# The last tile list takes 24 tiles in place of 18, and six early read-backs and their adds are issued inside the tail

## The reference

```python
def _L0_gnn_ref(h, adj, W_w, W_b, a):
    Wh = h @ W_w + W_b
    e = leaky_relu((Wh @ a1)[:, None] + (Wh @ a2)[None, :], negative_slope=0.2)
    attention = softmax(where(adj > 0, e, NEG), axis=1)
    return attention @ Wh
def _L0_ffn_ref(x, Wg, bg, W1, b1, W2, b2):
    topk_scores, topk_idx = top_k(x @ Wg.T + bg, 2)
    topk_probs = softmax(topk_scores)
    ...
    out = out + combine[..., e:e + 1] * (relu(x @ W1[e].T + b1[e]) @ W2[e].T + b2[e])
x = x + _L0_gnn_ref(_layernorm(x), adj, ...)
x = x + _L0_ffn_ref(_layernorm(x), ...)
```

## Time and profile before

| what | value |
|---|---|
| median of 3 runs | 413.72 us (413.57 to 413.85) |
| profiled execution, its own time | 413.95 us |
| its span | 412.2 us |
| TensorE busy | 383.2 us, 93% of the span |
| VectorE, ScalarE, GpSimd busy | 295.3, 270.1, 204.3 us |
| moved by DMA | 116.44 MB, mean 282 GB/s |
| granted TensorE clock, mean | 0.989 |

### The profile page before, as it was taken

How to read it: one execution, slowest core, us unless ns; L and a number is a source line. 1 busy time by engine, 2 the same in 40 slices (tenths; PEclk the granted TensorE clock), 3 DMA queues, 4 the chain that set the end, 5 groups by cost and what they waited for, 6 DMA issues and landing times.

```text
span 412.2 us, 8417 instructions
## 1 busy us (share of the span) xinstructions
PE 383.2 (93%) x2434; PEld 257.1 (62%) x2434; DVE 295.3 (72%) x819; ACT 270.1 (66%) x451; POOL 204.3 (50%) x247
## 2 busy tenths in 40 slices
PE   1899999999999999999999999999989999999960
PEld 1545555444444444444366667798879999999960
DVE  5998896989799979899988696268951692111173
ACT  1589879675878666892376975458646666676630
POOL 3283451100401874206763058789787777555560
PEclk9999999999999999999999999999999999999995
DMA  6999998969959999898676994576577777667795
GB/s 197 358 425 373 344 353 251 422 250 374 384 220 305 354 302 408 322 319 328 185 244 236 380 316 145 184 245 219 191 231 237 251 239 240 218 222 240 243 361 184
DMA packets 45610, 116.44 MB, mean 282 GB/s; under 512 B 7517, under 2 KB 19682, under 8 KB 38902
## 3 DMA queue, kind: packets, MB, share of 16 engines
q1 hardware_dynamic: 37062, 100.02, 68.0%
q0 software_dynamic: 4320, 8.47, 6.2%
q10 hardware_dynamic: 4176, 7.34, 5.9%
HBM read 84.57 MB, written 13.07 MB: 237 GB/s over the span
## 4 chain that ended last, share of the span: by engine, by line
PE 75%; DMA 8%; DVE 6%; issue 4%; SPq 3%; ACT 2%; POOL 2%; ACTq 0%; POOLq 0%; DVEq 0%
PE acc L1600 46%; PE acc L1702 10%; DMA adj<-adjT 3%; PE hps L1684 3%; PE hps L1686 3%; PE hps L1685 3%; PE yt L1702 3%; DVE prob L971 2%; PE yt L1645 2%; DMA ybuf<-wst,dest 1%; DMA adj<-ybuf 1%; PE pj L1721 1%; PE pj L1558 1%; SPq L547 1%; PE yt L1567 1%
## 5 line engine op out<-in xcount | busy, mean ns | idle before, releaser
L1600 PE MATMUL acc<-prob,Wh 128*128 128x512 f32 (+1 forms) x576 | 236.0, 550 | 3.8 <-DVE prob L971 2.7
L971 DVE SCALAR_TENSOR_TENSOR prob<-s_bc,E_col,G_all 128x1024 f32<-128x1024 f32 (+2 forms) x159 | 169.7, 1096 | 21.9 <-PE acc L1600 18.5
L1600 PEld LDWEIGHTS acc<-prob,Wh 128*128 128x128 f32 x576 | 103.5, 190 | 98.8 <-issue 84.2
L1355 ACT ACTIVATE G_all<-adj 128x2048 bf16<-128x2048 int32 (+1 forms) x67 | 119.0, 1800 | 22.7 <-DMA adj<-adjT 12.8
L784 POOL DMA_INDIRECT xbuf<-xr,slot x64 | 72.6, 1135 | 49.6 <-PE acc L1600 30.5
L800 POOL DMA_INDIRECT ybuf<-wst,dest x71 | 73.2, 1031 | 45.4 <-ACT wst L1438 25.0
L1702 PE MATMUL acc<-wall,prob 128*128 x368 | 51.1, 282 | 0.0
L1702 PEld LDWEIGHTS acc<-wall,prob 128*128 128x128 f32 x368 | 44.7, 192 | 0.2
L1223 DVE COPY share<-slab 128x1 f32<-128x1 f32 x45 | 6.8, 155 | 47.1 <-DMA slab<-xbuf 44.5
L1428 ACT ACTIVATE prob<-hps 128x512 f32<-128x512 f32 x46 | 27.6, 599 | 6.5 <-PE hps L1686 1.4
L1438 ACT ACTIVATE wst<-acc,share 128x128 f32<-128x128 f32 x45 | 16.6, 368 | 17.3 <-PE acc L1702 15.6
(11 more groups left out here) (249 smaller groups left out, 554.0 us busy)
## 6 DMA issues: line engine op xcount, KB each, us to landing
adj<-adjT SPq DMA_DIRECT2D x52, 1024.0 KB, 8.1
adj<-adjT SPq DMA_DIRECT2D x16, 768.0 KB, 6.2
s_bc<-wall SPq DMA_DIRECT2D x47, 256.0 KB
wlb<-wall SPq DMA_DIRECT2D x24, 256.0 KB
slab<-xbuf SPq DMA_DIRECT2D x71, 65.0 KB
adj<-ybuf SPq DMA_DIRECT2D x6, 512.0 KB, 7.7
xs<-x SPq DMA_DIRECT2D x8, 256.0 KB, 10.5
wst<-wcat ACTq DMA_DIRECT2D x8, 256.0 KB, 4.2
```

Source lines behind the costliest of these rows:

```text
L971: nc.vector.scalar_tensor_tensor(prob[n % PR][:, 0:w], c_bc[:, P * AT[g]:P * AT[g] + w], E_col[:, u:u + 1], G[m % GR][:, k * w:(k + 1) * w ...
L1355: nc.scalar.activation(G[m % GR][:, 0:w], adj_sb[m % AR][:, 0:w], ACT.Relu).then_inc(s_G, 1)
L1600: last = nc.tensor.matmul(bank[:, 0:k * P], Wh[:, u, :], prob[n % PR][:, b * P:(b + k) * P], start=(u == 0), stop=(u == TILES - 1), skip_g ...
```

## The change

The number of tiles in the list before the last goes from 12 to 6, so the last list begins with tile 47 and holds 24 tiles. `OLD` becomes the number of tiles that the first 24 blocks can fill at most, 55 in place of 61. The scratch table of the last list (24 by 24) moves to `G_all`, where the attention masks lay. The six early read-backs are issued by SyncE in its beats 60 to 65, one in each, behind that beat's slab and weight copy; the first one's wait for the given-back tiles goes with it. VectorE's adds for these parts are written into its beats 65 to 70.

```diff
     SURE = [-((E * (P - 1) - 2 * P * (AT[g] + WB[g])) // P) for g in range(SG - 1)]
     NT = (2 * N + E * (P - 1)) // P
     SURE[0] = 0
+    OLD = (2 * P * AT[SG - 2] + E * (P - 1)) // P
+    SURE[SG - 2] = OLD - E
+    assert OLD - E - SURE[SG - 3] >= 2 * AT[SG - 2] - SURE[SG - 3] - 1
     FIRST = [0] + SURE + [NT]
     CNT = [FIRST[r + 1] - FIRST[r] for r in range(SG)]
     MOST = max(CNT)
     CAP = N + P
     SPARE = NT - 2 * N // P
     C = 3 * E
-    OLD = FIRST[SG - 1] + E
     OLDER = (2 * P * AT[SG - 1] + E * (P - 1)) // P
     ROWS = E * CAP + SPARE * P
 
@@ -179,7 +181,8 @@
         WxT = WT
         full, acum = cut(0, E, TILES), cut(0, C, C)
...
-                       [cut(base, n, w) for base, n, w in ((544, MOST, E), (544, CNT[-2], 2 * E), (CNT[-1] * C, CNT[-1], C))])
+                       [cut(base, n, w) for base, n, w in ((544, MOST, E), (544, CNT[-2], 2 * E))])
+        pastq.append(G_all[:, 0:2 * CNT[-1] * C].bitcast(fp32).rearrange("p (a b) -> p a b", b=C))
...
-            def first_reads():
-
-                given_back(OLD)
-                for c in range(SOON):
-                    read_back(c)
+            def first_read(c):
+
+                if c == 0:
+                    given_back(OLD)
+                read_back(c)
...
                     for t in copies_at.get(n, ()):
                         copy_weights(t)
+                    for c in range(SOON):
+                        if n == beat_step[OLD + 5 + c]:
+                            first_read(c)
...
                 main(False)
-                first_reads()
...
-            def add_all():
-                for c in range(len(last_pass)):
+            def add_rest():
+                for c in range(SOON, len(last_pass)):
                     add_up(c)
...
                                 if t < NT:
                                     target(t)
+                            if 0 <= k - OLD - 10 < SOON:
+                                add_up(k - OLD - 10)
...
                 main(False)
-                add_all()
+                add_rest()
```

## The result

The changed kernel takes **416.78 us** (median of 8 runs, 414.83 to 418.99) against 413.71 for the kernel before (8 runs beside it, 412.51 to 414.78): the ratio is 1.0067, with a 95% interval of 1.0048 to 1.0087. It is slower by 0.5 to 0.9%. The forecast was 411.5; the kernel became slower, as rival (c) had it.

A forecast was written before the change was run, and what follows sets the result against it. TensorE was taken to bound the tail, then DMA work and a slow last give-back the final 14 us. From 413.72 us, -2.4 (end) + 0.2 (TensorE's wait) + 0 + 0 = -2.2 gave 411.5; range 410.3 to 413.4.

The forecast's parts named there:

- rival (c): Tail, slab 70 and copies behind it: TensorE starves and the kernel gets slower, 415.0 us; chance 0.08.
- The end, -2.4 us: After the last scaling: with early reads gone, the last two reads start at 403.0 instead of 405.4, gaining 2.4 us.
- The give-back is slow because of the six early read-backs: Tail's end: six reads issued from 387.16 on were said to make the give-back from 394.03 take 5.96 us.
- the median, 3.3 us: Last give-back: its landing time taken as the median of indirect writes without that load, range 2.5 to 4.7 us.
- rival (a): End: stores and ScalarE's three reads alone keep the last give-back at 5.3 us; 413.3 us, chance 0.13 together with (d), reads starting no earlier.
- TensorE's wait, +0.2 us: Turn of tile 70: its slab lands late behind four reads; TensorE waits 0 to 1.3 us once, taken as 0.2.
- near the lower end, because the SyncE queue itself goes slower: Tile 70's wait: 0.2 chosen from 0 to 1.3 us, since fewer rounds would be ahead of its slab.
- The rule of the Trainium skill: DMA queues: engines alternate between rows but take one row in ring order, so SyncE's slabs and copies wait behind reads.
- SyncE's issue times: Tail: wait for tile 54 costs nothing, first read issued about 378.5, last slab 386.5, all six reads by about 389.
- The adds: VectorE: six parts' adds, some 8.6 us, hidden before the next parts land from about 401 on; cost 0.
- The lists: Longer last table adds 1.1 us on VectorE, covered; slab 47's later wait costs 0, at most 1 us.
- the step on the earlier trace: Shorter table: VectorE feeds TensorE up to 0.7 us sooner, ending in the weight-copy wait at 303.44; counted 0.

The follow-up runs named there:

- e0: The changed kernel once more, unaltered, for a second profile; 416.49 us, ratio 1.0069 to the kernel before.
- e2: Changed kernel with all slabs up to tile 70 loaded ahead of the first early read-back; 416.66 us, ratio 1.0081 to the kernel before.
- e3: Changed kernel with the six early read-backs sent from ScalarE's DMA queue, one a beat, instead of SyncE's; 418.34 us, ratio 1.0112 to the kernel before.
- e7: Changed kernel without the six stores of the first 24 tiles; 416.69 us, ratio 1.0073 to the kernel before.
- e11: Changed kernel with early reads cut to an eighth of their bytes and the six early stores left out; 413.30 us, ratio 0.9986 to the kernel before.
- e12: Changed kernel with eighth-size early reads, no early stores, and ScalarE's three reads put behind the wait for tile 70; 414.63 us, ratio 1.0023 to the kernel before.
- e5: Changed kernel with all six early reads in place, each fetching only an eighth of its bytes; 413.20 us, ratio 1.0001 to the kernel before.
- e1: Changed kernel with the new lists kept but the six reads put back behind all SyncE's other work; 414.05 us, ratio 1.0002 to the kernel before.
- e9: Changed kernel with all six early reads in place, each fetching half of its bytes; 414.87 us, ratio 1.0015 to the kernel before.

## Why the prediction was wrong, point by point

**The end, -2.4 us: the step that failed first.** "*The give-back is slow because of the six early read-backs*" is the sentence; the estimate "*the median, 3.3 us*" followed from it. The step passed over the three reads on ScalarE's queue and the stores with "*It is not quite quiet*". With the six reads gone early the give-back still landed in 4.16 us in the changed kernel and in 3.5 to 4.8 in e0, e2, e3 and e7; e7 and e11 show that the three reads alone keep it at 4.5 to 4.7, and e12 that it takes 2.08 without them. Of the 1.1 us that the landing did give, 0.9 went into a later start and a longer stretch behind the last two reads, which the sum had taken as fixed at 6.8 us; the end gave 0.3 us at most. By the time, e5 bounds what the end is worth when the reads are nearly free: its interval allows 1.0 us of gain at most (0.25% of 413.7), and its ratio shows none. This is the mechanism of rival (a), which named the stores and the three reads together; e7 shows that it does not need the stores.

**TensorE's wait, +0.2 us: the term that was mis-sized.** The mechanism was right: reads of 1.47 us in beats with a quarter of the DMA time free, tile 70's slab short, landing between 390.8 and 392.2. In the first profile it was the only late one and landed within these bounds, shortly before 391.93. There the loss of 1.4 us is about the upper bound, 1.3. What was wrong was the choice inside them, "*near the lower end, because the SyncE queue itself goes slower*", and the bounds themselves: e0 and e3 show three late slabs each, the first of them tile 68's and tile 67's, and e2 a late weight copy (0.2 us) in place of a slab. In these profiles each transfer behind the reads could be late, not only the one that the forecast called the first to be short. By the times, e5 against the changed kernel (1.0001 against 1.0069 for e0; the intervals do not meet), the bytes cost 0.68%, about 2.8 us. That is past the 2.4 us at which the forecast's own rival (c) turns the sign, and there was no gain to use up first.

**Rival (c)** was given 0.08. It asked for 3.2 us of waits because these were set against a gain of 2.4; with an end that gives nothing a wait of 0.8 us, the least that the forecast could tell from none, makes the kernel slower. Its chance hung on the other term, and the text had no case in which both terms were wrong.

**The rule of the Trainium skill** that the forecast weighed gave the direction (slabs behind reads) but not the reason: in e3, with the reads on another row, slabs were as late.

**SyncE's issue times** were right: no wait of SyncE for tile 54 before 377.33, slab 70 at 386.71, all six reads by 389.0 (the first one 1.2 us sooner than the 378.5 worked out). **The adds** were hidden as forecast. **The lists**: cost 0, right (e1). TensorE's waits from 290 to 310 us, in the changed kernel:

```profile
PE acc L1606 <- DVE prob L975: 0.6, 1, 0.6
PE yt L1651 <- DMA slab<-xbuf: 0.5, 1, 0.5
PE hps L1690 <- DMA s_bc<-wall: 0.4, 1, 0.4
```

In the kernel before the first was 1.5 us and the copy's 0.2, with no slab waited for: what VectorE gave back sooner went into waits for DMAs, as the step on the earlier trace rows had said.

## What to carry to other kernels

A mean share of free DMA time is no budget: with 26% free, one early read of 524 KB cost nothing that could be told and two cost 0.35%, where the first late slab was the one right behind the second read. Before a late landing is charged to the largest traffic near it, list everything that goes in the same 3 us: here three reads of 262 KB on another queue, issued within 1.5 us of it, kept it at 4.5 to 4.7 us with the six of 524 KB long over or cut to an eighth and their stores left out. And when a gain and a loss in one sum are both estimates, ask for the loss at which the sign turns if the gain is zero.

## What the runs showed of the hardware that was not expected

A give-back of 128 rows landed in 2.08 us with nothing beside it (e12), and in 4.49 with three reads of 262 KB on another queue issued from 1.0 us before it to 0.4 after (e11), although the DMA share while it was on its way was 0.71:

```profile
400.50:404.50 4.00, 0.00 (x0) 0.00 (x0) 1.30 (x4) 0.00 (x0) 0.78 (x1) 0.59 0.71 224
```

In these two profiles a small indirect write took twice as long in company, with over a quarter of the engines' time still free.

Six whole reads on ScalarE's queue cost more (1.0112) than on SyncE's (1.0069). No run separates the reason; on SyncE the reads came more slowly (see e3), which may have acted as a brake.

One instruction packet took 2.05 us of one engine in e9. A packet of the same queue in the kernel before, from 392 to 394 us, took 3.2% of sixteen engines for 2 us, 1.0 us:

```profile
q8 instruction: 1, 0.02, 3.2%
```
